# A decoder layer on one core: a new table for the order in which eight streams of work are merged

## What is computed

```
x = layernorm(x + attn(x, Wqkv, Wo))          # 16 heads, 2 kv heads, width 128, rotary, softcap 30, causal
x = layernorm(x + xattn(x, ctx, mask, ...))   # 16 heads of width 16; wq and wo products on 8-bit integers
x = layernorm(x + ffn(x, Wr, br, W1, W2))     # 16 blocks of 64, of which each token keeps the best 4; gelu
```

## Time and profile before

| | |
|---|---|
| median of three executions | 386.93 us (385.92 to 387.41) |
| profiled execution, first to last instruction (span) | 382.7 us |
| profiled execution, its own time | not listed apart from the span; 4.2 us lie between the span and the median |
| PE busy | 370.5 us, 97% of the span |
| PE weight loads busy | 315.8 us, 82% |
| DVE busy | 293.5 us, 77% |
| ACT busy | 233.6 us, 61% |
| POOL busy | 151.0 us, 39% |
| granted clock of PE | full in all 40 slices of the span |
| chain that ended last | PE 80%, DVE 10%, issue 3%, DMA 3%, POOL 2%, ACT 1% |

### The profile page before, as it was taken

How to read it: one execution, slowest core, us unless ns; L and a number is a source line. 1 busy time by engine, 2 the same in 40 slices (tenths; PEclk the granted TensorE clock), 3 DMA queues, 4 the chain that set the end, 5 groups by cost and what they waited for, 6 DMA issues and landing times.

```text
span 382.7 us, 8976 instructions
## 1 busy us (share of the span) xinstructions
PE 370.5 (97%) x3038; PEld 315.8 (82%) x3038; DVE 293.5 (77%) x900; ACT 233.6 (61%) x494; POOL 151.0 (39%) x172
## 2 busy tenths in 40 slices
PE   8999999999999999999999999999999998999894
PEld 7678897978889888787998787989887897778783
DVE  2999888865688487899888868887878888976443
ACT  1658655545576865465686863867794455995240
POOL 4697947457544414454432332441302530000111
PEclk9999999999999999999999999999999999999999
DMA  8991753653524243124344221121121200000000
GB/s 283 367 345 57 249 174 75 189 169 84 166 84 109 88 137 113 46 75 155 111 109 140 57 57 40 47 82 57 45 82 48 79 2 2 15 16 2 0 30 27
DMA packets 21404, 38.42 MB, mean 100 GB/s; under 512 B 2544, under 2 KB 12144, under 8 KB 21360
## 3 DMA queue, kind: packets, MB, share of 16 engines
q1 hardware_dynamic: 20544, 37.06, 31.4%
q10 hardware_dynamic: 816, 0.79, 0.6%
HBM read 25.52 MB, written 5.24 MB: 80 GB/s over the span
## 4 chain that ended last, share of the span: by engine, by line
PE 80%; DVE 10%; issue 3%; DMA 3%; POOL 2%; ACT 1%; SPq 0%; POOLq 0%; DVEq 0%; ACTq 0%
PE acc L595 10%; PE bank L489 10%; PE bank L680 8%; PE bank L562 6%; PE bank L741 6%; PE bank L761 6%; PE bank L539 5%; PE bank L692 4%; PE bank L669 3%; PE bank L565 3%; PE bank L576 3%; PE bank L547 3%; PE bank L621 2%; PE bank L658 2%; PE bank L508 2%
## 5 line engine op out<-in xcount | busy, mean ns | idle before, releaser
L918 ACT ACTIVATE xs<-xs,xneg 128x256 f32<-128x256 f32 x128 | 53.5, 499 | 13.2 <-DVE xneg L1197 13.2
L1362 POOL TENSOR_TENSOR q_T<-q_T,rope_s 128x512 f32<-128x512 f32 x24 | 31.7, 1323 | 63.1 <-DMA rope_s<-rope_t 58.0
L1373 POOL TENSOR_TENSOR a_lo<-a_flat,a_hi 128x512 fp32r<-128x512 f32 x32 | 42.7, 1336 | 22.6 <-ACT a_flat L838 22.6
L595 PE MATMUL acc<-wo_s,a_hi 128*128 128x256 f32 x256 | 50.6, 296 | 0.0
L1197 DVE CUSTOM_DVE_ANT_0 xs<-bank,mask_s 128x256 f32<-128x256 f32 x128 | 45.7, 419 | 5.0 <-PE bank L669 4.6
L1391 POOL TENSOR_TENSOR small<-small,half 128x1 f32<-128x1 f32 x24 | 13.9, 584 | 75.9 <-DVE small L1081 75.9
L562 PE MATMUL bank<-v_s,p_near 128*128 128x129 f32 x256 | 42.0, 277 | 0.9 <-POOL p_near L1380 0.6
L595 PEld LDWEIGHTS acc<-wo_s,a_hi 128*128 128x128 f32 x256 | 39.4, 189 | 2.6 <-issue 2.6
L562 PEld LDWEIGHTS bank<-v_s,p_near 128*128 128x128 f32 x256 | 35.4, 191 | 5.1 <-issue 3.8
L489 PE MATMUL bank<-x_hi,wqkv_hi 128*128 128x256 f32 x124 | 38.6, 311 | 0.0
L595 PE MATMUL acc<-wo_s,a_lo 128*128 128x256 f32 x128 | 35.9, 280 | 0.0
(11 more groups left out here) (168 smaller groups left out, 970.1 us busy)
## 6 DMA issues: line engine op xcount, KB each, us to landing
wo_s<-wo_parts SPq DMA_DIRECT2D x24, 512.0 KB, 3.3
rope_s<-rope_t SPq DMA_DIRECT2D x54, 128.0 KB, 2.3
wo_parts<-wo_s SPq DMA_DIRECT2D x8, 512.0 KB, 3.3
xs<-in_wo SPq DMA_DIRECT2D x8, 256.0 KB, 5.8
stage<-in_wqkv SPq DMA_DIRECT2D x2, 512.0 KB, 5.1
xp_T<-in_wqkv SPq DMA_DIRECT2D x2, 512.0 KB, 6.9
y<-in_x SPq DMA_DIRECT2D x4, 256.0 KB, 3.1
ctx_s<-in_ctxT SPq DMA_DIRECT2D x4, 256.0 KB, 3.1
```

Of the source, the lines that this page charges most:

```text
L595: ins = mm(acc[:, t, :], a[x], wo_s[:, slot, w, m, :], start=(j == 0 and t == 0 and m == 0 and p == 0), stop=(j == PAIRS - 1 and m == 1 an ...
L918: activation(xs[:, t, m, m2, :], xs[:, t, m, m2, :], ACT.Exp, bias=xneg[:, t, m, m2:m2 + 1], scale=-1.0)\
L1362: g.tensor_tensor(dst, dst, (rope_s if b else rope_t)[:, n % 2], ALU.add).then_inc(sig["rotated", 0], 1)
L1373: g.tensor_tensor(a_lo[:, j % 2], a_flat[:, j % 2], a_hi[:, j % 2].bitcast(F32), ALU.subtract)\
```

## The change

Only `ORDER` is replaced by another string of the same 563 letters, each as often as before. No stream is changed inside. The file has 20 empty lines less at its top, so that line L1053 of the kernel before is L1033 of the changed one. The table in short:

```diff
 ORDER = (
-    "rrrmrrsmrmssrmrrsrmmmmrsssmmrmrmssmmmmmrrmmmmmmrmmmsssmcmmrrccmmmrmmcmcccmcccmmmssrrmccsmmmcmmmrsmxmmmssr"
...
+    "rrrrrmrsssmcrmrsmmrmrmmsrsrrmsmsmsmrrcmmmsmcmmmrmsmmmmmsmcccmmmrmmmrcmmcmmmrcmmsrcmrssmmmrmmrcymssmcmmmsy"
...
```

More of the change, by code:

```diff
@@ L152 @@
 ORDER = (
-    "rrrmrrsmrmssrmrrsrmmmmrsssmmrmrmssmmmmmrrmmmmmmrmmmsssmcmmrrccmmmrmmcmcccmcccmmmssrrmccsmmmcmmmrsmxmmmssr"
[L154 to L158, removed]
+    "rrrrrmrsssmcrmrsmmrmrmmsrsrrmsmsmsmrrcmmmsmcmmmrmsmmmmmsmcccmmmrmmmrcmmcmmmrcmmsrcmrssmmmrmmrcymssmcmmmsy"
+    "rmcmsrmsmxryscmxmsmmsmmxmmsmmrymmxrmyxrmxymymmxxsmyxymyxyxsmymxymrxyxymxyxymyxsxmxmyymxmmrrxxyymrsxymmxms"
+    "syyrrmmxscmmycxysmsmmcxmrmxmmssmmxyyxscxmccymmmmxmmxxymxrmnxmmynmyxyrrxxyymxxxymnyxxysyymxxyxrmyyxxysxysy"
+    "myxmrsxyyxcymmcxysymnmxrymxnncxcyrxcynmmysmxsycnoxymmxxmmyrsxxmyxmnyoyyymnxmosynxyyxxymmyxyxyxoyrsyxxyxyx"
+    "mymymxxsyxsnyxyxmmmmymmymxmmmxmccxmmnncmmnmycxmyxnxyccynyoxyxynyoynxxyyyxxoyxyxxyyyxxyyxxyxxoxyyyxxxnxyxy"
+    "ynnxnynyxynxxnnnnnonnnnoonoonnnnoonnon")
 def work_streams():
```

## The result

| | old table | new table |
|---|---|---|
| median | 386.43 us (385.50 to 387.41) | 404.09 us (400.52 to 408.01) |
| ratio, 95% interval | | 1.0442 (1.0381 to 1.0504) |
| profiled execution, its span | 382.7 us | 403.6 us, 401.9 us |

A forecast was written before the change was run, and what follows sets the result against it. PE was taken as a queue of work with few holes, opened where DVE or POOL hands over late. 3.3 - 1.4 - 1.3 + 0.6 = +1.2 us on the median of 386.93 us gave 388.1 us, range 385.3 to 391.0 us.

The forecast's parts named there:

- the new short distances: Places like `near`(1, 0), 8.2 us of PE work behind its rotation instead of 13.1: +0.6 us, ends 0 and 1.5.
- the rest of batch 0: Batch 0 after `mix`(0, 6): nothing more lost, second quantisation over some 1 us before PE wants it.
- the early quantisation: First cross weight quantised at 19.3 us delays `rot`(0, 7) and `proj`(0, 0): PE 3.3 us late by `mix`(0, 6), ends 2.3, 4.6.
- The holes at 79 to 87 us: PE's idle times around `mix`(1, 1) and `mix`(1, 4) close as weight work ends earlier: -1.4 us, ends 0 and -1.5.
- Single waits: Waits of `outproj`(0, 1) and `query`(3, 0) for a copy on ACT get filled with work: -1.3 us, ends 0 and -1.6.
- Jammed: Rival, slower: early quantisation meets POOL's densest stretch, DVE takes long values, `rot`(0, 7) ends after 38.4 us: +3.9, 390.8 us; chance 0.34.
- Absorbed: Rival, faster: early quantisation free for PE, slip under 1.1 us by `mix`(0, 6), gains stay: -2.0, 384.9 us; chance 0.13.
- The data of the cross weights: Rival: cross weights land later than DVE asks at 19.3 us, all of DVE stands: 3 us, 391 us; chance 0.03.
- What would show it wrong: Signs: `mix`(0, 6) before 39 us, or waits over half a us in several places behind 100 us.
- What would show it right: Signs: `mix`(0, 6) near 41.6 us, DVE without pause 19 to 45 us, no `mix` waits around 80 to 95 us.
- The base: Starting time: median 386.93 us, 4.2 us above the profiled span of 382.7 us, taken as lying outside it and unchanged.

The follow-up runs named there:

- the new start alone: The first 85 steps in the new table's order, the other 478 in the old order, against the old kernel: 1.0217, +8.3 us.
- the run that mends them in the old table: Old table, `outproj`(0, tile 1) moved behind `proj`(2, 2), `turn_k`(3, 3) between `turn_x`(3, tile 0) and its `query`: 1.0026 against the old kernel.
- with POOL short: Four POOL instructions (rotation sums, both low parts, bias) cut to 8 columns of each head or row: 0.9974 new table, 0.9914 old, against the old kernel.
- steps 207 to 271 alone: The old table with only steps 207 to 271 in the new order, against the old kernel: 1.0201, +7.7 us.
- the run of the one moved step: Old table with the first cross weight's quantisation moved right ahead of `rot`(0, 4), against the old kernel: 1.0169, +6.5 us.
- the second profile: Profile of the new table run again unchanged on another chip, against the old kernel there: 1.0476, 401.98 us.
- the run with `turn_w` later: New table with `turn_w`(0, 1) and two `w1` steps moved 11 steps on, 7.2 us of PE work later: 1.052 against the old kernel.
- quarters: New table, POOL's rotation sum and low part of attention each in four instructions of 128 columns, whole output: 1.0322 against the old kernel.

## Why the prediction was wrong

**The bound was right, the price of DVE's work was not.** PE is a queue with few holes, and DVE and POOL open them. What failed is that I priced DVE's instructions as durations of their own, from means and single rows, and left what happens when they meet POOL to a rival. By size the failed terms are the new short distances (+0.6 us forecast, 9.9 measured), the rest of batch 0 (nothing forecast, 4.7 measured) and the early quantisation (+3.3 us forecast, 5.7 measured).

*The early quantisation, forecast +3.3 us, measured 5.7 us.* The mechanism and the path were as told: `proj`(0, 0) waited for POOL behind the late rotation. It added only 0.4 us itself, since PE was 5.3 us late already, by smaller waits behind the same queue of DVE. Term by term: the quantisation took 5.15 us, not 3.6; so `rot`(0, 7) left DVE at 38.94 us, not 37.4, the same 1.5 us more. POOL's sum and low part took 1.80 and 1.72 us, not 1.27 each. Together 2.5 us, and `mix`(0, 6) stood at 44.08 us, not 41.6. All three are meetings. The ends, 2.3 to 4.6 us, took in only lengths that the old trace had shown, and a quantisation at a new place can meet POOL anew.

*"After that I see nothing more to lose in batch 0", measured 4.7 us.* I held the second quantisation, at 3.15 us, to be over 1 us before PE wants it. It took 6.6 us, and I had asked only when PE wants its result, not what else stands behind it in DVE's queue: PE stood 2.8 us for the product of `mix`(0, 8), whose bank `turn_w` takes. In this execution PE's clock fell behind the wait, 1.5 us that I had nowhere; with the new start alone it did not fall.

*The holes at 79 to 87 us, forecast -1.4 us, measured -1.9 us in this pair of traces.* Confirmed in the trace and worth nothing in the median: the exchange of steps 85 to 143 gave 1.0004, and the holes are not in every execution.

*Single waits, forecast -1.3 us.* They don't stand in the new list either, but the run that mends them in the old table gained nothing. A wait that is taken away by moving a step comes up again at whatever stood next.

*New short distances, forecast +0.6 us, ends 0 and 1.5.* Here some 9.9 us lie, from 175 us on, 1.3 of them with the low clock at 382 us. I had measured distances from the product that a quantisation reads, not from where the quantisation stands in DVE's queue: in the new table `quant_x`(1, tile 0), `scale2`(0, tile 1) and `quant_x`(1, tile 1) stand together right ahead of `turn_x`(1, tile 0), with no PE work between; in the old one 6 us. That short distance is the condition: with POOL short the same order costs nearly nothing. The price comes from the stretches of 1 us, which go straight into such a place, and from the clock behind it; steps 207 to 271 alone cost 7.7 us.

**The rivals.** *Jammed* named the mechanism and its point of decision, 38.4 us for `rot`(0, 7) against 38.94 measured, and its sign was right. Its price, +3.9 us, counted the start alone, as if the rule held only where POOL is dense; POOL needs only one instruction at the wrong time. A mechanism whose doubled instructions stood in the old trace should have been the forecast, applied to each place with a quantisation, and not to the start alone. *Absorbed* fell with the run of the one moved step. The data of the cross weights were there.

**What would show it wrong** did: `mix`(0, 6) came late, not early, 44.08 us against 41.6, but waits of over half a us stand in several places behind 100 us. PE's waits come to 17.7 us, not 8.5. What would show it right held for DVE without a pause up to 45 us, and for the holes.

**The base** was off as well, without changing the verdict. I took 4.2 us as lying outside the span. In every later run the time is 1.7 to 1.8 us above the span, so the old profile is, by estimate, of an execution of 384.4 us, faster than the median of its group. That is why PE is 19.1 us late between the two profiles and the medians are 17.7 us apart.

What stays open: how the last 3.7 us behind 200 us, less the 1.3 us of the low clock, divide between stretch and distance; why the clock falls in one execution and not in another; and why the holes at 79 to 87 us come and go.

## What to carry to other kernels

Where DVE and POOL share the work, a DVE instruction whose inputs all lie in SBUF costs its own length, or, where it falls into an instruction of POOL, the rest of that one and most of its own length on top; price it at both, at each place where PE waits for it. In an order written by hand, measure the distance to a consumer from where its producer stands in the producer's queue, count the release of the bank that it takes among its producers, and look for long instructions beside them on the other engine. A cheap probe is to halve the other engine's instructions: if that gains although the other engine gets slower, the loss is meetings, and whether it gains in the end is decided by whether that engine is waited for.

## What the runs showed of the hardware that I had not expected

- A DVE instruction on 2 numbers a row (0.17 us) took 1.07 us beside a POOL instruction of 1.28 us. The stand-still lasts to the end of POOL's instruction, and DVE's own work comes behind it: all 40 stretched instructions ended behind POOL's, by their own short length less 0.13 to 0.25 us.
- The form decides, not the load: DVE's instructions that read PSUM, its reductions and its reciprocals met POOL over 80 times and never stretched.
- Two of POOL's instructions of 0.77 us in place of one of 1.31 us, more time in all, made the new table 9.6 us faster. Between the halves DVE was let in nearly always; with quarters one DVE instruction stood through five of POOL's, 2.42 us.
- A long wait of PE often came with a fall of the clock, but not always. Waits of 2.8 us stand at granted clocks of 0.59 and 0.63 over 4 us in the first profile of the new table, 1.4 to 1.5 us more each. The same wait at 57 us left the clock at 1.00 in the run of the new start, and a wait of 2.77 us at 192 us did so in the run with `turn_w` later. At 175 us a wait of 1.24 us left it at 1.00, while one of 1.42 us in the second profile was followed by 0.65.
- The same old kernel ran at 386.4 us in one group of runs and at 383.7 to 384.5 us in five others, and a wait of 0.65 us that one profile shows was missing in others. A term of that size from one trace is not a gain.
